# Attention by four heads in 32-partition row groups, maximum subtracted through an extra row

## The reference

```python
k = _ln(k, kln_w, kln_b); q = _ln(q, qln_w, qln_b)      # 16 heads of 16 columns
dot = jnp.einsum('bqhs,bkhs->bhqk', q, k) * scalefactor
dot = jnp.where(causal, -jnp.inf, dot)
attn = jax.nn.softmax(dot, axis=-1)
out = jnp.einsum('bhqk,bkhs->bqhs', attn, v).reshape(b, t, e)
return out @ Wu.T
```

## Time and profile before

| | |
|---|---|
| Median of 3 runs | 5941.73 us (5937.52 to 5945.01) |
| Span of the profiled execution | 5941.4 us |
| PE, PEld busy | 4404.2 us (74%), 2798.0 us (47%) |
| DVE, ACT, POOL busy | 4376.5 us (74%), 2750.8 us (46%), 2791.5 us (47%) |
| Mean granted clock of TensorE | 0.895 |

### The profile page before, as it was taken

One profiled execution on the slowest core, in us unless ns is written; L12 is line 12 of the kernel. 1 busy time (PEld: TensorE's weight loads), 2 busy tenths in 40 slices (PEclk: granted clock), 3 DMA queues, 4 the chain that ended last, 5 costly groups with the idle time before them and its releaser, 6 DMA issues. The chain is left out here.

```text
span 5941.4 us, 54580 instructions
## 1 busy us (share of the span) xinstructions
PE 4404.2 (74%) x15853; PEld 2798.0 (47%) x15853; DVE 4376.5 (74%) x6879; ACT 2750.8 (46%) x5566; POOL 2791.5 (47%) x2070
## 2 busy tenths in 40 slices
PE   6887777877778787777877777787777877777732
PEld 4554444554444545445554444545445554444511
DVE  4439678695877959588695877959588695877976
ACT  3445453544535445453554535445354544535432
POOL 1226446362553726346362553736346372643733
PEclk9999898989989898898998989898898989989865
DMA  4401102020110201001020110201001020110200
GB/s 178 172 29 47 36 18 68 1 71 15 39 47 8 68 12 57 29 22 65 1 75 12 43 44 8 68 12 61 26 22 65 4 71 12 43 43 8 68 4 4
DMA packets 69368, 248.54 MB, mean 42 GB/s; under 512 B 9456, under 2 KB 9840, under 8 KB 68592
## 3 DMA queue, kind: packets, MB, share of 16 engines
q1 hardware_dynamic: 68976, 243.67, 11.9%
HBM read 212.19 MB, written 31.46 MB: 41 GB/s over the span
## 5 line engine op out<-in xcount | busy, mean ns | idle before, releaser
L1183 DVE TENSOR_TENSOR_SCAN hb<-a_bar,hb 128x512 f32<-128x512 f32 x768 | 1334.7, 1793 | 0.0
L1244 POOL TENSOR_TENSOR kept<-kept,hb 128x512 f32<-128x512 f32 x768 | 1017.5, 1358 | 441.7 <-DVE hb L1190 441.7
L903 ACT ACTIVATE room<-ps,row_min 128x128 f32<-128x128 f32 (+3 forms) x1024 | 540.4, 528 | 1099.4 <-DVE row_min L963 1098.4
L963 DVE CUSTOM_DVE_ANT_0 ps<-ps,causal 128x128 f32<-128x128 f32 (+3 forms) x1024 | 505.0, 493 | 670.8 <-PE ps L818 669.0
L767 POOL TENSOR_SCALAR room<-room,head_mask 128x512 f32<-128x512 f32 x208 | 345.0, 1659 | 1114.4 <-PE ps L818 1073.2
L1124 ACT ACTIVATE a_bar<-kept,a_neg 128x512 f32<-128x512 f32 x768 | 517.2, 718 | 710.1 <-DVE hb L1183 605.2
L818 PE MATMUL ps<-room 128*128 128x128 f32 (+3 forms) x2048 | 742.0, 446 | 96.1 <-ACT room L903 63.3
L840 PE MATMUL ps<-room 128*128 128x512 f32 (+3 forms) x2048 | 731.3, 443 | 0.8 <-issue 0.8
L1043 PE MATMUL ps<-hid_bhi,wring 128*128 128x512 f32 x1536 | 660.6, 430 | 95.4 <-POOL hid_blo L1230 44.5
L829 PE MATMUL ps<-ident,room 128*128 128x128 f32 x2560 | 472.6, 284 | 276.0 <-ACT room L903 274.5
L1043 PE MATMUL ps<-hid_ahi,wring 128*128 128x512 f32 x1280 | 567.7, 444 | 111.7 <-POOL hid_alo L1230 111.5
(11 more groups left out here) (179 smaller groups left out, 7673.7 us busy)
## 6 DMA issues: line engine op xcount, KB each, us to landing
wring<-w_hi SPq DMA_DIRECT2D x352, 512.0 KB, 3.2
kept<-in_wffn SPq DMA_DIRECT2D x22, 512.0 KB, 4.2
w_hi<-wring SPq DMA_DIRECT2D x22, 512.0 KB, 2.7
w_lo<-wrest SPq DMA_DIRECT2D x22, 512.0 KB, 2.9
xn<-in_x_fm SPq DMA_DIRECT2D x17, 512.0 KB, 3.2
out_fm<-xc SPq DMA_DIRECT2D x16, 512.0 KB, 2.6
room<-in_wmod SPq DMA_DIRECT2D x2, 1536.0 KB, 7.9
win<-in_win SPq DMA_DIRECT2D x1, 1024.0 KB, 8.9
```

Source lines behind the costliest of these rows:

```text
L903: act.activation(probs[:, h % 2, TRI[j]:TRI[j + 1]], bank(n % 2)[:, 0:(j + 1) * P], ACT.Exp, bias=row_min[:, n:n + 1], scale=-1.0, accum_o ...
L963: dve.tensor_tensor_reduce(bank(n % 2)[:, 0:w], bank(n % 2)[:, 0:w], causal[:, T - w:T], 1.0, 3.0e38, ALU.add, ALU.min, row_min[:, n:n + 1 ...
L1183: dve.tensor_tensor_scan(hb[:, s % 8, :], a_bar[:, s % 6, :], hb[:, s % 8, :], 0.0, ALU.mult, ALU.add).then_inc(scanned, 1)
L1244: pool.tensor_tensor(acc[:, m, :], acc[:, m, :], hb[:, s % 8, :], ALU.add).then_inc(acc_done, 1)
```

## The change

The attention of `part_a` is rewritten. Heads are taken four at a time (`quad`), each in its own 32 partitions: head g's 16 rows stand in partitions 32g and up, in `q_ver` and `k_ver` (one version for even heads and one for odd ones), with an extra row that is 1 in k. A loop of 15 slots takes the place of 72 sub-steps; slot k holds group u = k % 3 of quad k // 3.

- `scores`: four products with 32 contraction rows, head g into bank g, and four products that add the causal mask on the diagonal block (`ident_r`, `causal_r`, both float32r). `find_max`: one reduction over the four banks for each query tile, negated, written to `row_max`.
- `turn_max` transposes the maxima, `shift_q` adds them to q's extra row. The product with k's row of ones then subtracts them.
- `scores_turned`: the scores again, with k stationary, so that they come out keys by queries, in the same banks 0 to 3. `exp_probs`: one exponential for four heads. The transposes of probabilities and their copies are gone, as is the accumulated row sum.
- POOL zeroes what lies beyond the diagonal (`affine_select`). `values` multiplies with `v_pad`, 32 columns a head: 16 of v and one of ones, which gives the row sum; head g goes to partitions 32g and up of bank 4.
- At the end four output tiles are turned, the sums are inverted and spread by 16 transposes, and `wu` has four row blocks, half of each zero: eight products of 512 columns.
- The 72 side steps are dealt to the slots in halves (`halves(k, i)`); their contents are unchanged.

```diff
+QUADS = 4
+S_GROUPS = [[(3, 0)], [(2, 0), (0, 384)], [(1, 0)]]
+T_GROUPS = [[(0, 0)], [(1, 0), (3, 384)], [(2, 0)]]
+G_WIDTH = [512, 512, 256]
...
+        SLOTS = 3 * (QUADS + 1)
...
+            def halves(k, i):
+                s = 2 * k + i
+                return range(STEPS * s // (2 * SLOTS), STEPS * (s + 1) // (2 * SLOTS))
...
+                    def causal_probs(quad, u):
+                        for j, at in T_GROUPS[u]:
+                            pool.wait_ge(exp_done, 3 * quad + u + 1)
+                            blk = probs[u][:, :, at:at + P]
+                            pool.affine_select(blk, blk, [[0, 4], [1, P]], ALU.is_ge, 0.0, base=0, channel_multiplier=-1).then_inc(p_masked, 1)
+
+                    for k in range(SLOTS):
+                        for q in halves(k, 0):
+                            side_pool(pool, q, fin, pre)
+                        if k >= 3:
+                            causal_probs(k // 3 - 1, k % 3)
+                        for q in halves(k, 1):
+                            side_pool(pool, q, fin, pre)
...
+                    def scores(quad, u):
+                        c, p = quad // 2, quad % 2
+                        if u == 0 and quad >= 1:
+                            pe.wait_ge(q_shifted, quad)
+                        elif quad >= 1:
+                            pe.wait_ge(exp_done, 3 * (quad - 1) + u)
+                        elif u >= 1:
+                            pe.wait_ge(max_ready, u)
+                        for i, at in S_GROUPS[u]:
+                            w = (i + 1) * P
+                            for g in range(4):
+                                r = slice(32 * g, 32 * g + 32)
+                                pe.matmul(bank(g)[:, at:at + w], q_ver[r, p, c, i * P:(i + 1) * P], k_ver[r, p, c, 0:w], start=True, stop=False)
+                            for g in range(4):
+                                mm = pe.matmul(bank(g)[:, at + i * P:at + w], ident_r[:, :], causal_r[:, :], start=False, stop=True)
+                        mm.then_inc(s_done, 1)
+
+                    def scores_turned(quad, u):
+                        c, p = quad // 2, quad % 2
+                        if quad + 1 < QUADS:
+                            pe.wait_ge(max_ready, 3 * (quad + 1) + u + 1)
+                        elif u >= 1:
+                            pe.wait_ge(exp_done, 3 * quad + u)
+                        if u == 0:
+                            pe.wait_ge(q_shifted, quad + 1)
+                        for j, at in T_GROUPS[u]:
+                            w = T - j * P
+                            for g in range(4):
+                                r = slice(32 * g, 32 * g + 32)
+                                mm = pe.matmul(bank(g)[:, at:at + w], k_ver[r, p, c, j * P:(j + 1) * P], q_ver[r, p, c, j * P:T], start=True, stop=True)
+                        mm.then_inc(st_done, 1)
...
+                    def values(quad, u):
+                        pe.wait_ge(p_masked, 4 * quad + (1, 3, 4)[u])
+                        if u == 0 and quad >= 1:
+                            pe.wait_ge(o_copied, quad)
+                        for j, at in T_GROUPS[u]:
+                            w = T - j * P
+                            for g, h in enumerate(heads_of(quad)):
+                                mm = pe.matmul(bank(4)[32 * g:32 * g + 32, j * P:T], v_pad[:, j, h, :], probs[u][:, g, at:at + w],
+                                               start=(j == 0), stop=(j == 2))
+                        mm.then_inc(pv_done, 1)
+
+                    pe.wait_ge(ones_set, 1)
+                    for k in range(SLOTS):
+                        quad, u = k // 3, k % 3
+                        if quad < QUADS:
+                            scores(quad, u)
+                        for q in halves(k, 0):
+                            side_pe(pe, q, *side)
+                        if k >= 4:
+                            values((k - 1) // 3 - 1, (k - 1) % 3)
+                        if quad >= 1:
+                            scores_turned(quad - 1, u)
+                        for q in halves(k, 1):
+                            side_pe(pe, q, *side)
+                        if u == 2 and quad < QUADS:
+                            turn_max(quad)
...
+                    def exp_probs(quad, u):
+                        act.wait_ge(st_done, 3 * quad + u + 1)
+                        if quad >= 1:
+                            act.wait_ge(pv_done, 3 * (quad - 1) + u + 1)
+                        act.activation(probs[u], ps[:, 0:4, 0:G_WIDTH[u]], ACT.Exp).then_inc(exp_done, 1)
...
+                    def find_max(quad, u):
+                        p = quad % 2
+                        dve.wait_ge(s_done, 3 * quad + u + 1)
+                        for i, at in S_GROUPS[u]:
+                            cols = row_max[:, p, i, :].rearrange("p (g r) -> p g r", r=32)[:, :, HS * (1 - p)]
+                            ins = dve.tensor_reduce(cols, ps[:, 0:4, at:at + (i + 1) * P], AX.X, ALU.max, negate=True)
+                        ins.then_inc(max_ready, 1)
...
+                    for k in range(SLOTS):
+                        if k // 3 < QUADS:
+                            find_max(k // 3, k % 3)
+                        side_steps(k, 0)
+                        side_steps(k, 1)
+                        if k % 3 == 2 and k // 3 < QUADS:
+                            shift_q(k // 3)
```

More of the change, by code:

```diff
@@ L770, in _ @@
-                    for h in range(3 if att else 0):
-                        head(h)
-                    for q in range(STEPS):
-                        if att and q % TT == 0 and q // TT + 3 < HEADS:
-                            head(q // TT + 3)
-                        side_pool(pool, q, fin, pre)
+                    if not att:
+                        for q in range(STEPS):
+                            side_pool(pool, q, fin, pre)
+                        return
+                    pool.memset(v_pad.rearrange("p a b c -> p (a b c)"), 0.0).then_inc(pads_clear, 1)
@@ L852, in _ @@
[L852 to L853 removed]
+                    pe.wait_ge(ver_act, 4)
+                    pe.wait_ge(ver_dve, 4)
+                    def scores(quad, u):
[14 more added lines that the diff above has]
+                        mm.then_inc(s_done, 1)
@@ new lines, in _ @@
+                    values(QUADS - 1, 2)
+                    pe.wait_ge(exp_done, 3 * QUADS)
+                    for quad in range(QUADS):
+                        pe.wait_ge(o_copied, quad + 1)
+                        for i in range(TT):
+                            mm = pe.transpose(bank(quad)[:, i * P:(i + 1) * P], o_sb[:, quad, i * P:(i + 1) * P], ident[:, :])
+                    mm.then_inc(o_turned, 1)
+                    pe.wait_ge(o_summed, 1)
+                    for quad in range(QUADS):
+                        for i in range(TT):
+                            mm = pe.transpose(bank(quad)[:, i * P:(i + 1) * P], o_rep[:, quad, i, :], ident[:, :])
+                        mm.then_inc(o_spread, 1)
@@ L854, in _ @@
+                    for quad in range(QUADS):
+                        pe.wait_ge(o_normed, quad + 1)
                         for m in range(DC):
-                            mm = pe.matmul(bank(2 + m), wu[:, c, m * P:(m + 1) * P], o_t[c], start=(c == 0), stop=(c == DC - 1))
-                            if c == DC - 1:
+                            mm = pe.matmul(bank((4, 0)[m]), wu[:, quad, m * P:(m + 1) * P], o_sb[:, quad, :], start=(quad == 0), stop=(quad == QUADS - 1))
+                            if quad == QUADS - 1:
@@ new lines, in copy_out, with side_steps @@
+                    def copy_out(quad):
+                        act.wait_ge(pv_done, 3 * (quad + 1))
+                        act.activation(o_sb[:, quad, :], bank(4), ACT.Copy).then_inc(o_copied, 1)
+                    def side_steps(k, i):
+                        for q in halves(k, i):
+                            side_act(act, q, *side)
+                            if first:
+                                split_act(act, q)
+                    for k in range(SLOTS):
+                        side_steps(k, 0)
+                        if k >= 6 and k % 3 == 0:
+                            copy_out(k // 3 - 2)
+                        if k >= 3:
+                            exp_probs(k // 3 - 1, k % 3)
+                        side_steps(k, 1)
@@ new lines, in shift_q, with side_steps @@
+                    def shift_q(quad):
+                        c, p = quad // 2, quad % 2
+                        dve.wait_ge(max_turned, quad + 1)
+                        dve.tensor_tensor(q_ver[:, p, c, :], q_ver[:, p, c, :], bank(0), ALU.add).then_inc(q_shifted, 1)
+                    def side_steps(k, i):
+                        for q in halves(k, i):
+                            side_dve(dve, q, *side)
+                            if first:
+                                split_dve(dve, q)
@@ new lines, in _ @@
+                    for k in range(SLOTS):
```

(16 more changed lines are left out.)

245 lines of the change are left out of this document (75 added, 170 removed).

## The result

The changed kernel takes 6048.05 us (median of 4 runs, 6046.92 to 6051.34) against 5939.62 us for the kernel before on the same chip: 1.0182 times as long, 95% interval 1.0168 to 1.0196, or 108 us slower. The forecast was 6020 us, slower. The result is inside the range, but two terms of the forecast were wrong in opposite directions, as the stages show.

The account below looks back on a forecast made before the run. It saw two limits in part A: attention's chain with TensorE's side matmuls, then a full VectorE. Full passes +6.1 x 14 = +85, pass 1 +3, pass 0 -10, together +78 on 5941.4: 6020 us, range 5840 to 6300.

Parts of the forecast that it names:

- The ring through four banks: Attention loop: scores, maximum, transposed scores, exponential strictly in turn through the same banks; 25.2 us per quad against 28 before.
- VectorE's scan work: Slots 9 to 14 of a full pass: VectorE sets the pace, 55.2 us.
- the maximum: VectorE's reduction over four banks: 2.3, 2.4 and 1.2 us for the three groups of a quad.
- the exponential: ScalarE's one operation for four heads: 1.95, 1.95 and 1.05 us for the three groups of a quad.
- four heads of 512 columns cost 2.15 us: TensorE's row-group products: each head overlaps only the second record of the one before, five records of 0.43 us.
- four at once: Rival: four row groups run together on TensorE, 0.87 us a group, saving 9.5 us a pass; 5870 us, chance 0.22.
- the clock: Tail of a full pass: 2.0 us (0 to 9) added for 16 records at a TensorE clock that climbs again.
- low clock throughout: Rival: the tail's 16 records and 36 transposes cost 9 us, 7 over the count, 15 times; 6125 us, chance 0.14.
- The sum of the tail: From VectorE's last scan product to the residual: 19.3 us, 14 more than before, without the 2.0 for the clock.
- Pass 0, forecast 10 us shorter: Pass with only attention in its loop: 120 us against 131, taken as -10 since weight splitting shares the loop.
- The causal products: Mask products of 128 columns in the scores: 0.06 us each, plus 0.16 for emptying the array before them.
- The selection: GpSimd's 16 causal selections of 512 columns: 1.3 us each (0.6 to 2.1), hidden except at the end.

Follow-up runs that it names:

- e1: Changed kernel with a block of TensorE test products, full, row-group and column-group, before pass 0; only this block is read; the run of 6158.16 us contains it.
- e7: Changed kernel with two unused full products after the scores and two after the transposed scores, in all slots of pass 0: 6035.00 us.
- e8: Changed kernel with the same unused products as e7, but in slots 6 to 10 of the passes with side work: 6001.79 us.
- e3: Changed kernel with four unused full products of 512 columns ahead of the last values, in passes with side work: 5995.40 us.
- e2: Changed kernel with GpSimd's last causal selection put ahead of the last four scan sums: 5949.17 us.
- e4: Changed kernel without the products that add the causal mask, so the row maximum covers the whole diagonal block: 5919.07 us.
- e5: Changed kernel with e2's order and a shorter end: sums spread by one product per quad, inverted on ScalarE, quads 0 to 2 in slots 13 and 14: 5902.42 us.
- e6: Changed kernel with the short end of e5 and without causal products before the maximum as in e4: 5771.63 us.
- e9: e6 with the unused products of e7 (slots 0 to 11 of pass 0) and e8: 5709.42 us.
- e10: e5 with the spreading and inverting of the sums of quads 0 to 2 put behind the loop: 5912.77 us.
- e11: e9 with one more SyncE wait, so part B's three weight tiles are requested at the loop's first scores: 5711.48 us.

## Why the prediction came out as it did

**What was right.** The ring through four banks and its order; that the pass would be attention's ring first and VectorE's scan work after; the maximum (2.3 forecast, 2.29 measured), the exponential (1.95, 1.88), part B unchanged, slots 12 to 14 with GpSimd's sums ahead of the last selection. That part A came out at 194.8 us against 194 is luck: slots 3 to 8 are 5.5 us shorter than forecast, and the other stages 6 us longer.

**The step that failed first: four heads of 512 columns cost 2.15 us.** I argued that the two records of a head need the same rows and starts are in order, so that only one can overlap. They cost 0.91 us (e1), 1.07 in the kernel at the high clock. That is the rival "four at once", and in slots 3 to 8, mostly at the high clock, it shows: 58.9 us instead of 64.4. By the sum of that rival alone the kernel would have been faster, 5870 us.

**The step that failed second: the clock.** I allowed 2.0 us for it in the tail and nothing elsewhere. The change takes work off TensorE between waits (no transposes, scores at a quarter of the time), and the granted clock went to 0.50 to 0.54 in pass 0, 0.58 in slots 9 to 11 and 0.50 in the first 14 us of the tail. With unused products the kernel gains 13, 46 and 53 us (e7, e8, e3). These don't simply add: 1.9 of e8's 3.1 us a pass are in the tail, which e3 speeds up too. Counted once, the clock is worth some 53 + 13 + 15 x 1.2 = 84 us, an estimate from three runs, since the three were not run together. In slots 9 to 11, raising it from 0.58 to 0.80 gained nothing (e8). Nor is the clock the one thing that decides: GpSimd's order alone is worth 99 us (e2), and the causal products 129 (e4). In the tail the cost was 3.5 us a pass by e3, where I had 2.0 and the rival "low clock throughout" 9: the transposes ran at 0.50, the output products at 0.85. The sum of the tail had two more errors that offset each other in part: the first sixteen transposes at 0.6 us (3.7, since all of them stand behind the last values) and the 2,048-column copy at 1.9 (1.23).

**Pass 0, forecast 10 us shorter, is 12 longer.** At the high clock it is 6 shorter than before (e7: 215.8 against 221.8). Of the miss of 22 us, 18 are the clock.

**The causal products** were taken at 0.40 us a group with the emptying; they cost 0.50 at the high clock and 1.05 at the low one, nearly all of it on the path in pass 0 and in slots 0 to 8, a quarter of it after that (e4).

**The selection** was taken at 1.3 us and took 0.61 to 0.64 for one of 512 columns. That it stands behind the sums in the tail was in the sum, and e2 shows its price: 6.6 us of each part A.

The total was thus near for a poor reason: too dear an array, too high a clock. What stays open is what holds TensorE and VectorE at the start of part A in e5, e6, e9, e10 and e11. Their waits end 1.0 to 1.7 us after a packet of instructions has landed, which points to the supply of instructions, but no run tests that; the tiles are part of VectorE's delay in e9, and in e5 and e10 it was not tested. Why the clock falls where it does is not settled either. Unused full products bring it back, so what TensorE is given decides it. But the busy share alone does not order the stretches (62% busy at 0.81 in slots 6 to 8, 68% at 0.58 in slots 9 to 11, where the low clock itself lengthens the busy time), and in e1 the clock fell with TensorE busy all the time on one row group. Whether products that leave rows of the array unused count for less in the kernel too, no run here shows.

## What to carry to other kernels

Packing products into row groups makes TensorE's share of a ring short, and its clock can then fall from 2.4 to 1.2 GHz, as it did here; read the granted clock of each stretch, and price products at both levels before counting the gain. A low clock costs time only where TensorE is on the path. In a ring through the same banks a small operation costs nearly its full length as long as the ring sets the pace, so take out those (here the mask) before making large ones faster. When two gains seem to add up, compare them stage by stage. In a tail, look at each engine's order: 0.6 us of work behind 5 us of sums held everything.

## What the runs showed of the hardware that was not expected

- Four float32 products of 512 columns in four row groups: 0.91 us together, one full product 0.87. One row group repeated: 0.86 us a product at clock 1.00, like a full one.
- During that repetition the granted clock fell to 0.50 with TensorE busy without a gap; full products brought it back to 1.00 (e1).
- Four column groups do as well: 3.57/4 = 0.89 us for four products of 128 rows and 32 output columns (L1329 in e1).
- Unused products made the changed kernel faster in three places, by 13 to 53 us, and e6 by 62. Raising the clock from 0.58 to 0.80 in slots 9 to 11 gained nothing there.
- The same first instruction of a block starts 2.7 to 3.1 us (e2) or 6.1 to 8.7 us (e10) after the same event in two kernels whose blocks differ only at their end. In both, 1.0 to 1.7 us before it a DMA packet of instructions has landed, the first of the part in e2 and the second in e10.
